# Loads of the stored activations issued by ScalarE on its own DMA queue, inside a spectral convolution

## What is computed

```python
h = _gconv1x1(h, fc0_w, fc0_b)
for i in range(4):
    h1 = _spectral_conv(h, sp_w1[i], sp_w2[i])   # rfft2, mix 24 x 12 modes, irfft2
    h2 = _gconv1x1(h, w_w[i], w_b[i])
    h = h1 + h2
    if i < 3:
        h = _gswish(h, betas[i])
h = _gswish(_gconv1x1(h, fc1_w, fc1_b), betas[3])
return _gconv1x1(h, fc2_w, fc2_b)
```

## Time and profile before

| | |
|---|---|
| median of 3 runs | 3180.91 us |
| the profiled execution's own time | 3186.44 us |
| its span, first to last instruction | 3184.4 us |
| mean granted TensorE clock | 0.918 |
| PE busy | 2694.4 us (85%) |
| DVE busy | 2009.1 us (63%) |
| ACT busy | 1366.5 us (43%) |
| POOL busy | 1028.1 us (32%) |
| queue q1 (issued by SP) | 384.22 MB |
| queue q10 (issued by ACT) | 31.46 MB |
| passes 0 to 31 of the spectral layers | about 1100 to 2430 us of the span |

### The profile page before, as it was taken

One profiled execution on the slowest core, in us unless ns is written; L12 is line 12 of the kernel. 1 busy time (PEld: TensorE's weight loads), 2 busy tenths in 40 slices (PEclk: granted clock), 3 DMA queues, 4 the chain that ended last, 5 costly groups with the idle time before them and its releaser, 6 DMA issues. The chain is left out here.

```text
span 3184.4 us, 47373 instructions
## 1 busy us (share of the span) xinstructions
PE 2694.4 (85%) x18156; PEld 2102.5 (66%) x18156; DVE 2009.1 (63%) x2535; ACT 1366.5 (43%) x2365; POOL 1028.1 (32%) x1050
## 2 busy tenths in 40 slices
PE   0599997877968398969999999999997599999568
PEld 0244443435645287868888889888886588888345
DVE  6988876767843633226656666666754389888633
ACT  1777775653222122223333333334242376776322
POOL 2988800225513201102020100111111177777410
PEclk9999998998979699689989999999988699999779
DMA  8300003558332345388887979797976735461134
GB/s 210 84 0 26 13 13 98 165 152 194 76 112 63 60 122 128 115 212 213 199 223 197 218 199 217 212 219 223 211 200 191 131 62 102 69 108 18 64 97 102
DMA packets 242229, 423.48 MB, mean 133 GB/s; under 512 B 85931, under 2 KB 188971, under 8 KB 217155
## 3 DMA queue, kind: packets, MB, share of 16 engines
q1 hardware_dynamic: 224251, 384.22, 50.7%
q10 hardware_dynamic: 17280, 31.46, 2.9%
q0 software_dynamic: 496, 5.01, 0.4%
HBM read 252.61 MB, written 166.38 MB: 132 GB/s over the span
## 5 line engine op out<-in xcount | busy, mean ns | idle before, releaser
L1580 ACT ACTIVATE fno_act<-fno_pz 128x320 f32<-128x320 f32 x512 | 225.8, 442 | 702.7 <-PE fno_pz L1498 691.7
L1245 DVE STREAM_TRANSPOSE spec_chan<-spec_form_in 128x1024 f32<-128x1024 f32 x256 | 497.5, 1954 | 22.8 <-DMA spec_form_in<-table_iw_t 22.8
L1447 POOL TENSOR_SCALAR fno_xm<-fno_xm 40x384 f32<-40x384 f32 x96 | 116.3, 1211 | 1043.0 <-DMA fno_xm<-scratch_modes 1043.0
L1498 PE MATMUL fno_pz<-spec_cols,spec_chan 128*128 128x96 f32 x3072 | 398.0, 284 | 0.0
L1856 POOL TENSOR_TENSOR head_hact_lo<-head_hact,head_hact_hi 128x512 fp32r<-128x512 f32 x256 | 342.8, 1362 | 154.8 <-DVE head_hact_hi L2002 152.7
L1498 PEld LDWEIGHTS fno_pz<-spec_cols,spec_chan 128*128 128x128 f32 x3072 | 371.6, 197 | 18.4 <-issue 11.0
L1528 PE MATMUL fno_pw<-fno_fw,fno_act 128*128 128x96 f32 x2560 | 307.7, 280 | 37.5 <-DVE fno_wfreq L1712 32.9
L1528 PEld LDWEIGHTS fno_pw<-fno_fw,fno_act 128*128 128x128 f32 x2560 | 297.4, 195 | 46.4 <-DVE fno_wfreq L1712 39.6
L610 PE MATMUL cml_acc<-cml_logis,cml_mats 128*128 128x512 f32 x480 | 247.1, 596 | 56.1 <-DVE cml_logis L567 56.1
L1549 PE MATMUL fno_pj<-fno_xm,fno_wt 128*40 128x32 f32 x4608 | 242.2, 218 | 50.2 <-DVE fno_om L1735 26.9
L1549 PEld LDWEIGHTS fno_pj<-fno_xm,fno_wt 128*40 128x40 f32 x4608 | 219.9, 135 | 71.0 <-issue 55.2
(11 more groups left out here) (219 smaller groups left out, 4962.0 us busy)
## 6 DMA issues: line engine op xcount, KB each, us to landing
scratch_form<-fno_act SPq DMA_DIRECT2D x32, 2560.0 KB, 10.3
spec_form_in<-scratch_form SPq DMA_DIRECT2D x64, 1024.0 KB
scratch_mixed<-fno_om ACTq DMA_DIRECT2D x192, 160.0 KB
fno_wt<-table_mix_w SPq DMA_DIRECT2D x192, 150.0 KB
fno_coef<-scratch_mixed SPq DMA_DIRECT2D x48, 480.0 KB, 8.8
nca_raw<-scratch_xnp SPq DMA_DIRECT2D x66, 329.7 KB
spec_form_in<-scratch_form SPq DMA_DIRECT2D x32, 512.0 KB
scratch_modes<-fno_both SPq DMA_DIRECT2D x32, 360.0 KB, 11.4
```

Of the source, the lines that this page charges most:

```text
L1245: return nc.vector.transpose(chan[:, to * TR * PIX:(to + 1) * TR * PIX].rearrange("p (h q w) -> p h q w", h=TR, q=4), src)
L1498: mm = nc.tensor.matmul(pz[:, t % 4, m * 96:(m + 1) * 96], left, cols[:, h * CS:h * CS + 96] if layer else wz[:, :], start=m == 0, stop=Tr ...
L1580: nc.scalar.activation(act_b[:, :, 4 * t:4 * t + 4], z, ACT.Silu if n >= UNITS else ACT.Copy).then_inc(a_out, 1)
```

## The change

SP no longer issues the form loads of the passes. ACT does, on its own queue (q10), at the end of the same passes, n = 6 to 31: behind the last two mixed stores where the pass has them, and ahead of the fill of `spec_cols` and of `cols_out`. The source, the destination, the sizes and the semaphore that counts their landing are the same. ACT now waits for the transposes of pass n and for the form store of pass n - 6 before it issues them. SP keeps its wait for the transposes and the loads of `iw_t`. The head after the passes still loads its units by SP.

```diff
--- before.py
+++ after.py
@@ -1424,7 +1424,6 @@
                             sp.dma_start(form_in[0:32, old, :], k["iw_t"][0]).then_inc(iw_in, 16)
                             sp.dma_start(form_in[32:64, old, :].rearrange("p (q f) -> p q f", q=4)[:, :, 0:16 * H],
                                          k["iw_t"][1].rearrange("p (q f) -> p q f", q=4)[:, :, 0:16 * H]).then_inc(iw_in, 16)
-                        load_unit(sp, form_in, old % 2, form[old // UNITS % 2, old % UNITS], unit_in[old % 2])
                 begin_mix(SIDES - 1)
                 first_modes(SIDES - 1)
                 for m in last_mix:
@@ -1617,6 +1616,12 @@
                                 store_mixed(m - 2)
                     for m in mixed_in(n)[-2:]:
                         store_mixed(m)
+                    if n + 2 >= UNITS:
+                        old = n + 2 - UNITS
+                        if n >= UNITS:
+                            act.wait_ge(turned, (n - UNITS + 1) * NT8)
+                        act.wait_ge(act_stored, 16 * (old + 1))
+                        load_unit(act, form_in, old % 2, form[old // UNITS % 2, old % UNITS], unit_in[old % 2])
                     if n % UNITS == UNITS - 1:
                         act.wait_ge(scaled, LAYERS)
                         act.wait_ge(z_done, (n + 1) * NZ)
```

## The result

The changed kernel took 3281.43 us (median of 4 runs, 3259.79 to 3290.56), the kernel before, on the same chip, 3184.78 (4 runs, 3178.32 to 3199.05). The ratio is 1.0287 with a 95% interval of 1.0225 to 1.035: **slower by 2.3 to 3.5%**. I had forecast 3213 us, with a range up to 3258: the right side, and far too little.

The account below looks back on a forecast made before the run. PE, busy 85% of the span, was taken to bound the passes. Terms +40, +8, -23 and +7 gave +32 us on the profiled 3186.44, so 3218, carried to the runs' median as 3213 us; range 3168 to 3258.

Parts of the forecast that it names:

- h = 2.1: Assumed time in us that three form-load issues hold ACT at each of 24 pass ends, ahead of the inverse-row evictions.
- under 1.6 and over 3.7: Sums in us of ACT's three form-load issues that would show the assumed 2.1 wrong.
- my +40: Cost in us of ACT's hold at 24 pass ends, 12 x 1.21 + 12 x 2.1, with PE waiting for evictions.
- my bounds of 26 and 79: Cost in us of ACT's hold at pass ends, with issues of 1.54 or of 3.74 us.
- The clock at pass ends, +8: PE's longer pause at 12 mix-pass ends makes its clock fall: 1.4 us at half of them, +8 us.
- my bound of 17: Upper bound in us for the cost of clock falls at the ends of the 12 mix passes; the lower was 0.
- The mixed stores' stall, -23: In mode products of n % 4 = 1, stores no longer meet the form load's tail: -23 us, bounds -33 and 0.
- Start of layer 1, +7: Pass 7's form load now runs beside the inverse table, which DVE waits for: +7 us, bounds -4 and 11.
- Rival 1: No stall goes away or it moves, as to late modes at first products in three passes: 3236 us, chance 0.15.
- the 4.7 of my sum: PE's idling in us at the first product of three passes if the whole form load precedes the modes' tail.

Follow-up runs that it names:

- the run with the hold alone: Kernel before, no transfer moved, ACT kept busy about 4 us by eight small copies before the inverse-row evictions in 12 passes: 3245.44 us, ratio 1.0221.

## Why the prediction was wrong

- **Which step failed: "I take h = 2.1, midway between 1.54 and 2.70".** One h stood for 24 ends. The runs show two kinds: 1.28 us without mixed stores (0.36 us of PE, not 1.21) and 3.5 to 5.2 with them, 4.1 in the mean; I had named under 1.6 and over 3.7 as signs of being wrong. At the first kind the loads go out ahead of the form store, at the second behind it and behind ACT's own mixed stores. I had set the rows with a form store ahead (2.70 and 3.74) half aside because that store was on the same queue; with one under way on the other queue, and nothing on its own, ACT was held 1.46 to 3.65 us. And I left the mixed stores' own part out of h, though a single one took 1.71 us in the earlier trace rows. PE's wait rose by 57.5 us for my +40, inside my bounds of 26 and 79.
- **The clock at pass ends, +8, was also too small.** Passes 9 to 31 lost 59.8 us net; adding the 16.1 gained back gives 75.9. Less the 57.5 of waiting, 18.4 are left, past my bound of 17. I priced falls at 1.4 us for every second end; in the changed kernel each of the 12 passes behind them has a mean clock of 0.91 to 0.95, and the run with the hold alone lost 70 us for 43.8 of waiting.
- **The mixed stores' stall, -23: right cause, 16 us of it seen.** DVE's wait for them is gone, and passes 13, 17 and 21 took 49.9, 49.7 and 50.3 us at full clock; pass 29 took 53.0 at 0.94. Passes with n % 4 = 1 gained 16.1 us; their successors' share is buried in the hold. The Trainium skill, *DMA: Bandwidth & Descriptors*, section "Issuing engines are not separate DMA queues", allows only issue time to be saved; here passes got shorter, not by another issuer as such but by an earlier place.
- **Start of layer 1, +7: right cause, too small.** The table came 5.9 us later (28.74 for the 22.82 of the earlier trace rows); passes 7 and 8 took 12.4 us more. The run that gives these loads back to SP has pass 8 shorter by 13.5. Over all profiles, passes 7 and 8 took 84 to 87 us together where SP issues these loads and 90 to 99 where ACT does.
- **Rival 1 stayed away here, by little.** First products in five passes waited 0.57 to 1.83 us. From 2.73 on such a pass costs some 19 us more, not the 4.7 of my sum. Four of the experiments fell into it without my meaning it.
- **Open.** The passes account for +72.2 us (59.8 and 12.4) from pass 7 to pass 31; the medians differ by 96.6, with an interval of some 72 to 111 (0.0225 and 0.035 of 3184.78). The execution profiled of the changed kernel lost 18.5 us ahead of the first moved load, which no experiment tied to the change; the end of pass 0 and the time of pass 6 vary like this in kernels with the same program up to there. What the other runs lost there is not known. The terms of my sum came to 57.5 + 18.4 - 16.1 + 12.4 = 72.2 us for the +32 forecast, each on the dear side.

## What to carry to other kernels

Price a DMA issue by what is under way at that moment, on the issuing engine's own queue and on the others, and ask what stands behind it in that engine's program: the same three issues cost PE 0.36 us at one end and 6.14 at another. When a transfer is moved, look for the loads with little slack that it now meets; a first product 2.73 us late cost some 19 us. Where a change helps at some places and hurts at others, do it only there: the same move at the right 9 of 26 ends, with one chunk of modes ahead, was 0.3 to 0.75% faster than before, not 2.9% slower.

## What the runs showed of the hardware

- Three DMA issues on ACT (2.62 MB) took 1.28 us where neither its own queue nor SP's had a store just ahead, 1.46 to 3.65 with only SP's queue at work, a form store 4.5 to 7.8 us ahead, mostly 2.2 to 3.2 behind mixed stores of its own with the form store coming after, and 3.5 to 5.2 us behind both. At five single ends of pass 27 or 28, in five kernels, they took 2.2 to 3.2 us without either just ahead; no run shows why.
- After PE idled 2.73 us or more at the first product of a pass, its granted clock was 0.50 (1.2 GHz) for nearly all that was left of the pass, though PE was busy (64.91 of 68.50 us in one such pass); after 2.17 us or less at this place it stayed at 1.00 (2.4 GHz) just behind. That is no limit for other places: 1.78 us later in pass 13 of the kernel before were followed by 0.50. At the pass ends, behind a hold of ACT, 4 to 6 us of idling were followed by only some 4 to 10 us at the low level, as the mean clocks of the passes behind say (0.95 in 37.47 us, 0.91 in 55.11).
